# Two blocks of 40 unread products on TensorE, ahead of the first transposes and the first score stacks of an attention stage

## The reference

```
def _L2_attn_ref(x, W_attn, W_proj):
    qkv = x @ W_attn
    q, k, v = jnp.split(qkv, 3, axis=2)          # each to 4 heads of 32
    att = jnp.einsum('bhqd,bhkd->bhqk', q, k) * scale
    att = jnp.where(causal, att, jnp.finfo(att.dtype).min)
    att = jax.nn.softmax(att, axis=-1)
    y = jnp.einsum('bhqk,bhkd->bhqd', att, v)
    ...
    return y @ W_proj
...
t = t + _L2_attn_ref(_ln_t(t), L2_attn_W_attn, L2_attn_W_proj)
```

## Time and profile before

| what | value |
|---|---|
| median of three runs | 2985.64 us (2984.97 to 2986.77) |
| the profiled execution | 2989.96 us, its span 2988.3 us |
| TensorE, products | 2548.2 us busy, 85% of the span |
| TensorE, weight loads | 1943.9 us, 65% |
| VectorE | 1948.2 us, 65% |
| ScalarE | 1464.9 us, 49% |
| GpSimd | 1438.2 us, 48% |
| mean granted clock of TensorE | 0.907 |

### The profile page before, as it was taken

One profiled execution on the slowest core, in us unless ns is written; L12 is line 12 of the kernel. 1 busy time (PEld: TensorE's weight loads), 2 busy tenths in 40 slices (PEclk: granted clock), 3 DMA queues, 4 the chain that ended last, 5 costly groups with the idle time before them and its releaser, 6 DMA issues. The chain is left out here.

```text
span 2988.3 us, 63601 instructions
## 1 busy us (share of the span) xinstructions
PE 2548.2 (85%) x21349; PEld 1943.9 (65%) x21349; DVE 1948.2 (65%) x4075; ACT 1464.9 (49%) x2354; POOL 1438.2 (48%) x1108
## 2 busy tenths in 40 slices
PE   5478896663799999999999999999999999996191
PEld 3256664452577777777777777777777777775070
DVE  3756764685576676776767767767677677674215
ACT  1124453231455655656656566566565665664030
POOL 0204572000265745747557457475574574753424
PEclk7597897866899999999999999999999999997595
DMA  2021110013122021121220211212202112121134
GB/s 104 0 46 45 43 44 9 7 52 82 33 47 50 19 58 30 39 58 27 46 51 19 58 30 39 58 27 46 51 19 58 30 40 58 27 45 41 42 112 65
DMA packets 83320, 131.10 MB, mean 44 GB/s; under 512 B 15296, under 2 KB 56640, under 8 KB 82928
## 3 DMA queue, kind: packets, MB, share of 16 engines
q1 hardware_dynamic: 72368, 112.69, 15.1%
q0 software_dynamic: 4816, 12.13, 2.0%
q10 hardware_dynamic: 5904, 2.71, 0.3%
HBM read 59.85 MB, written 16.00 MB: 25 GB/s over the span
## 5 line engine op out<-in xcount | busy, mean ns | idle before, releaser
L2364 ACT ACTIVATE a_PT<-PS 128x512 f32<-128x512 f32 x1079 | 632.1, 600 | 525.6 <-PE PS L2238 402.0
L2100 POOL TENSOR_TENSOR a_KT<-a_PT 128x512 f32<-128x512 f32 (+1 forms) x241 | 430.2, 1794 | 134.5 <-ACT a_PT L2364 111.9
L2100 POOL TENSOR_TENSOR a_KT<-a_KT,a_PT 128x1024 f32<-128x1024 f32 x192 | 403.6, 2102 | 47.6 <-ACT a_PT L2364 35.0
L2429 DVE TENSOR_REDUCE a_NM<-PS 128x2 fp32r<-128x512 f32 x460 | 301.3, 685 | 146.7 <-PE PS L2190 140.9
L2237 PE MATMUL PS<-a_QH,a_K 128*128 128x256 f32 (+1 forms) x1280 | 374.5, 319 | 0.0
L2088 POOL TENSOR_TENSOR a_TM<-a_R 128x256 f32<-128x256 f32 x306 | 217.7, 736 | 303.1 <-DVE a_R L2399 303.1
L2237 PE MATMUL PS<-a_QH,a_KSW 128*128 128x256 f32 (+1 forms) x1232 | 362.0, 323 | 0.0
L2443 DVE TENSOR_REDUCE a_MX<-PS 128x1 f32<-128x512 f32 (+3 forms) x432 | 273.0, 666 | 125.0 <-PE PS L2204 71.3
L2238 PE MATMUL PS<-a_QL,a_K1B 128*128 128x256 f32 (+1 forms) x1280 | 325.7, 280 | 0.0
L2201 PE MATMUL PS<-a_K,a_QH 128*128 128x512 f32 (+3 forms) x768 | 260.7, 397 | 0.0
L2237 PEld LDWEIGHTS PS<-a_QH,a_K 128*128 128x128 f32 x1280 | 246.1, 192 | 15.9 <-issue 6.6
(11 more groups left out here) (430 smaller groups left out, 5893.1 us busy)
## 6 DMA issues: line engine op xcount, KB each, us to landing
a_KWB<-a_KSW SPq DMA_DIRECT2D x68, 256.0 KB, 3.2
a_K1B<-a_K SPq DMA_DIRECT2D x32, 512.0 KB, 5.5
a_XC<-latents SPq DMA_DIRECT2D x17, 512.0 KB, 3.6
a_CKS<-latents SPq DMA_DIRECT2D x17, 512.0 KB, 4.6
a_CF<-latents SPq DMA_DIRECT2D x17, 448.0 KB, 4.2
c_EX<-in_experts SPq DMA_DIRECT2D x1, 4608.0 KB, 18.2
a_WK<-in_wk SPq DMA_DIRECT2D x17, 256.0 KB, 4.5
a_KSW<-a_KSW SPq DMA_DIRECT2D x17, 256.0 KB, 5.1
```

What stands on the lines that cost most here:

```text
L2100: nc.gpsimd.tensor_tensor(total, one_in, other_in, ALU.add).then_inc(s["added"], 1)
L2364: nc.scalar.activation(PT[:, u, to:to + HALF], turning(key), ACT.Exp).then_inc(s["taken"], 1)
L2429: ins = nc.vector.tensor_reduce(out, bank.rearrange("p (a n) -> p a n", a=2), AX.X, ALU.max, negate=True)
```

## The change

A function `keep_clock` issues 40 products of the identity with the three masks, 384 columns each, into `P[7]`, with no wait and no semaphore. TensorE calls it twice: ahead of `tx.0.0`, whose wait is for the normed tokens of image 0, and ahead of `far.0.0.0`, whose wait is for the two stacks of image 0. Nobody reads what they write. No other engine's program is touched.

```
@@ stage_attn2, TensorE's program @@
+                def keep_clock():
+
+                    for _ in range(40):
+                        nc.tensor.matmul(P[7][:, 0:384], identb[:, :], masks.rearrange("p a n -> p (a n)"), start=True, stop=True)
+
                 def turn_tokens(st):
                     _, b, half = st
...
                 for st in course.steps:
                     what = st[0]
+                    if st == ("tx", 0, 0) or st == ("far", 0, 0, 0):
+                        keep_clock()
                     if st == ("qk", 0, 0, 0):
```

## The result

The changed kernel takes 2947.56 us (median of four runs, 2943.94 to 2952.49), the kernel before 2985.3 us in the runs beside it (four, 2978.01 to 2986.77): a ratio of 0.9879 with an interval of 0.9855 to 0.9904, 37.7 us less. Forecast were 4.2 us less. The profiled execution took 2944.21 us, with a span of 2942.5 us.

What follows compares the result with a forecast made beforehand. TensorE at half clock was taken to bound the chain to the first stack copy and the 32 us from `far.0.0.0`. Savings of 2.06 + 2.1 = 4.2 us from 2985.64 gave 2981.4 us, 8-in-10 range 2971.0 to 2985.5.

Steps and rivals of the forecast that it cites:

- the rival of the lasting clock: From `far.0.0.0` on, full clock also shortens the following 23.70 us, saving 9.5 us more: 2971.9 us, chance 0.33.
- Whether the clock lasts: At the eleven `far` steps: clock falls during or right behind them, so the following 23.70 us stay at 1.2 GHz.
- The first block: Ahead of `tx.0.0`: 6.8 us, hidden behind VectorE's norm with 0.2 us to spare; first stack copy 2.06 us earlier.
- The rival of slow blocks: At both waits, blocks run at 1.2 GHz, 12.8 us each, 11.9 us late together: 2997.5 us, chance 0.06.
- The second block: Ahead of `far.0.0.0`: ends at 221.8 to 223.4 against 223.25, hidden or late by 0.2 us at most.
- The first score stacks: Eleven `far` steps ahead of the first `score` step: 6.3 us at full clock instead of 8.43, saving 2.1 us.

Runs made afterwards that it cites:

- The code alone: Changed kernel with neither block, 80 unread products of 8 columns in the convolution stage instead, 160 instructions added against the kernel before: 2963.94 us, ratio 0.9924.
- the second block alone: Changed kernel with only the block ahead of `far.0.0.0`, plus 40 unread products of 8 columns in the convolution stage: 2953.00 us, ratio 0.9884 against the kernel before.
- The first block alone: Changed kernel with only the block ahead of `tx.0.0`, plus 40 unread products of 8 columns in the convolution stage: 2962.40 us, ratio 0.9913 against the kernel before.

## Why the prediction was wrong

**The missing term: the place of later code, about -25 us.** The working costed the 80 products as time on TensorE at two waits and said that behind them everything waits for events, "so the saving reaches the end". It never asked what 160 more instructions do to a loop further down. The profile of before had the signs: branches of 2.5 us, and 15 waits for issue of 18.7 us together in `stage_heads`. No rival named it. The code alone gives -23.9 us, and this is the larger part of the 37.7. It is also why the time lies far below the whole range of 2971.0 to 2985.5: the rival of the lasting clock, 2971.9 us, less the 24.7 us of the loop is 2947.2, against 2947.56 measured.

**"Whether the clock lasts": wrong; the rival's case came true.** The step took it that the clock falls once during or right behind the eleven `far` steps. It weighed them as work in pieces, 4.7 us in 6.3, and compared them with 209.20 to 213.00, busy for half. In the trace TensorE is busy for 5.58 of their 5.80 us, and the clock stands at 1.00 through them and the 28.5 us behind. The rival's steps were right in kind. From `far.0.0.0` to the end of the long stretch it expected 2.1 + 9.5 = 11.6 us; the second block alone gave 10.9, and with both blocks the stage is 12.0 shorter. With half the block, and 3.4 us of rest before the steps, the clock was lost as the forecast had it for the whole block. So the eleven steps alone don't decide it: what stands ahead of them does, the rest or the amount of work.

**The first block: hidden by 0.2 us in the forecast, 1.2 us late in the trace.** 40 products were to take 6.8 us at full clock. The clock fell as they began, they took 8.34, and the transposes start 8.23 us after the stage's first DMA instead of 7.07 (201.23 - 194.16). The block does bring the clock back before the transposes, which run in 1.04 us and not 1.97. From them to the first copy of a stack it is 200.93 - 196.21 = 4.72 us, just what the working gave. What it had wrong is the clock at which the block starts: with the 1.16 us of delay, the chain from first DMA to first copy goes from 13.85 to 12.95 us, -0.9 in place of -2.06. The first block alone moved the median by 1.5 us, within the spread. The rival of slow blocks had the direction of this right, and its sign, a first block of over 7.0 us, came true; its price, 5.8 us late, would have needed the low clock for the whole block.

**The second block: right in price and in being hidden.** 0.17 us a product were taken, 6.66/40 = 0.167 measured. It starts 23.2 us after the stage's first DMA, where the working had 20.8 to 22.4, and still ends as the stacks are ready: 200.93 plus the 17.30 us that passed before from first copy to `far.0.0.0` (208.01 to 225.31) is 218.23, and the step starts at 218.03.

**The first score stacks: right in kind, small in size.** 6.3 us were expected in place of 8.43, at the pace of VectorE. They take 223.78 - 218.03 = 5.75: the eleven reductions follow each other without a gap (6.13 us), the first 0.98 us after the first product.

**The rest, not assigned.** Of the -45.8 us of span, -6.2 lie before the stage and -2.8 between it and the loop, and both vary by themselves; against the medians, -24.7 and -12.0 make -36.7 of the measured -37.7. That the sum comes so near is in part luck: the stage without blocks took 261.8 to 270.5 us by profile, so the 12.0 could have been 8 to 17, while with both blocks it took 254.0, 253.3 and 253.9.

## What to carry to other kernels

Before costing an edit that adds or removes instructions, look for a hardware loop behind it in the same engine's stream: a branch back of microseconds and waits for issue at the head of a pass were here the signs that its place in the code costs. 32, 80 and 96 unread products ahead of it took 25 us off the loop without any block, more than the blocks gave, and 112 added 25: such an edit has to be measured at several sizes. To judge what an edit does, compare it with a kernel that has the same number of instructions and not the edit. Filling a wait of TensorE right before its next long stretch with unread products can keep the clock through that stretch, if the filling reaches to its start; half of it, which left 3.4 us of rest, gave nothing here.

## What the runs showed of the hardware

- A branch back of TensorE's loop of about 2,400 instructions a pass takes 0.36 to 0.47 us or 2.5 to 3.5 us (medians), depending on how many instructions stand ahead of it; two pairs of kernels 256 apart agree (1799.9 and 1802.8 us, 1775.2 and 1775.3 us for 15 passes), at a granted clock of 1.00 before and after. The two ends of the table are 49.3 us apart in the loop.
- With the clock lost, 30 to 32 us at 1.2 GHz follow although TensorE is busy throughout (30.00 of 30.00 us); with the same work started from full clock, 28.5 us are run at 2.4 GHz, busy for 27.96.
- The clock fell to 0.50 as the first block began, stood there from 189 to 191 and was 1.00 again from 192, during the block, so that its 40 products cost 8.34 us instead of 6.66.
